# A transformer block on one core: products of probabilities and values in pairs, full-width transposes of the maxima, and a new order of stages

## The reference

```
x = x + 0.5 * ffn(layernorm(x))
x = x + attn(layernorm(x))
x = x + 0.5 * ffn(layernorm(x))

attn: q = rope(x @ Wq + bq); k = rope(x @ Wk + bk); v = x @ Wv + bv
      out = softmax(q k^T / 4) v per head; out @ W0 + b0
ffn:  base = x @ W_base + b_base
      h_n = relu(x @ W_enc[n] + b_enc[n]); recon_n = h_n @ W_dec[n] + b_dec[n]
      n* = argmin over n of mean((recon_n - x)^2)
      mid = relu(x @ W_down[n*] + b_down[n*]); out = base + mid @ W_up[n*] + b_up[n*]
```

## Time and profile before

| | |
|---|---|
| median of 3 runs | 1844.04 us (1842.85 to 1847.05) |
| the profiled execution | 1842.72 us |
| its span on the core | 1840.9 us |
| mean granted TensorE clock | 0.976 |
| PE busy | 1739.8 us |
| DVE busy | 1286.3 us |
| ACT busy | 978.3 us |
| POOL busy | 497.6 us |

### The profile page before, as it was taken

How to read it: one execution, slowest core, us unless ns; L and a number is a source line. 1 busy time by engine, 2 the same in 40 slices (tenths; PEclk the granted TensorE clock), 3 DMA queues, 4 the chain that set the end, 5 groups by cost and what they waited for, 6 DMA issues and landing times.

```text
span 1840.9 us, 26466 instructions
## 1 busy us (share of the span) xinstructions
PE 1739.8 (95%) x9128; PEld 987.3 (54%) x9128; DVE 1286.3 (70%) x2795; ACT 978.3 (53%) x1954; POOL 497.6 (27%) x665
## 2 busy tenths in 40 slices
PE   6478999999999999999999999999999999999976
PEld 4343555555555555555556555555556555554434
DVE  5459686867768676776868677686867768686521
ACT  1126465655646565564646556474655637465531
POOL 2415041231414123141413214050322405032101
PEclk9689999999999999999999999999999999999996
DMA  4334231233333123333322333332233333214000
GB/s 117 58 59 79 43 52 37 45 69 58 70 58 53 38 41 67 58 70 58 58 36 51 54 59 69 58 61 39 52 46 58 70 58 61 46 41 69 18 12 12
DMA packets 96715, 99.38 MB, mean 54 GB/s; under 512 B 19972, under 2 KB 88261, under 8 KB 96453
## 3 DMA queue, kind: packets, MB, share of 16 engines
q1 hardware_dynamic: 93830, 97.16, 29.9%
q10 hardware_dynamic: 2752, 0.54, 0.2%
HBM read 63.54 MB, written 33.55 MB: 53 GB/s over the span
## 4 chain that ended last, share of the span: by engine, by line
PE 81%; DVE 11%; issue 2%; ACT 2%; DMA 2%; POOL 1%; SPq 0%; POOLq 0%; ACTq 0%; DVEq 0%
PE ps L725 11%; PE ps L784 10%; PE ps L737 10%; PE ps L713 10%; PE ps L800 10%; PE ps L802 6%; PE ps L842 5%; PE ps L858 4%; DVE mx L1088 4%; PE ps L843 3%; PE ps L824 3%; PE ps L868 2%; PE ps L769 2%; DVE xn L1119 2%; PE ps L889 1%
## 5 line engine op out<-in xcount | busy, mean ns | idle before, releaser
L1088 DVE TENSOR_REDUCE mx<-ps 128x1 f32<-128x512 f32 x1024 | 656.8, 683 | 287.2 <-PE ps L713 284.9
L940 ACT ACTIVATE pr<-ps 128x512 f32<-128x512 f32 x1024 | 556.2, 597 | 543.0 <-PE ps L725 541.9
L725 PE MATMUL ps<-stack 98*128 98x512 bf16 x1024 | 312.5, 384 | 7.9 <-ACT pr L940 2.4
L713 PE MATMUL ps<-stack 96*128 96x512 bf16 x1024 | 310.9, 381 | 4.7 <-DVE mx L1088 4.1
L737 PE MATMUL ps<-pr,va 128*32 128x512 f32 x2048 | 273.3, 604 | 1.2 <-ACT pr L940 1.1
L725 PEld LDWEIGHTS ps<-stack 98*128 98x128 bf16 x1024 | 73.9, 98 | 234.8 <-issue 158.1
L713 PEld LDWEIGHTS ps<-stack 96*128 96x128 bf16 x1024 | 99.0, 98 | 136.1 <-DVE mx L1088 30.6
L1315 POOL CAST wdh<-wd_all 128x128 fp32r x32 | 9.5, 296 | 555.9 <-DVE adapter L1169 499.9
L1141 DVE SCALAR_TENSOR_TENSOR ps<-ps,wb,h 128x512 f32<-128x512 f32 x128 | 96.8, 756 | 77.0 <-PE ps L802 76.9
L1250 POOL TENSOR_SCALAR rs<-mv 128x4 f32<-128x4 f32 x48 | 11.5, 239 | 471.6 <-DVE mv L1108 467.7
L1279 POOL TENSOR_TENSOR qb<-qb,cst 128x512 f32<-128x512 f32 x64 | 98.6, 1541 | 136.9 <-DVE qs L1195 136.9
(11 more groups left out here) (151 smaller groups left out, 2991.9 us busy)
## 6 DMA issues: line engine op xcount, KB each, us to landing
stack<-scratch SPq DMA_DIRECT2D x384, 128.0 KB, 6.1
scratch<-parts SPq DMA_DIRECT2D x64, 384.0 KB, 2.6
xin<-in_L_attn_x_dram SPq DMA_DIRECT2D x16, 512.0 KB, 4.4
out_dram<-x SPq DMA_DIRECT2D x16, 512.0 KB, 5.2
stack<-wu_mT SPq DMA_DIRECT2D x128, 4.0 KB, 1.7
cst<-in_const_dram SPq DMA_DIRECT2D x1, 1024.0 KB
raw<-in_L_ffn_W_dec_dram ACTq DMA_DIRECT2D x1, 512.0 KB, 5.6
pr<-in_L_ffn_W_enc_dram SPq DMA_DIRECT2D x2, 256.0 KB, 7.7
```

What stands on the lines that cost most here:

```text
L713: pe.matmul(bank1[:, t % 2, :], stack[0][0:KB, hd, 128 * t:128 * t + 128], stack[1][0:KB, hd, :], start=True, stop=True).then_inc(s1_full. ...
L725: pe.matmul(bank2[:, a % 2, :], stack[1][:, 4 * g + a, 128 * t:128 * t + 128], stack[0][:, 4 * g + a, :], start=True, stop=True).then_inc( ...
L940: act.activation(pr[:, n % 2, a, :], bank2[:, a % 2, :], ACT.Exp, scale=SCALE).then_inc(ex_done.sem, 1)
L1088: dve.tensor_reduce(mx[:, hd // 4 % 2, e:e + 1], bank1[:, t % 2, :], AX.X, ALU.max).then_inc(mx_done.sem, 1)
```

## The change

- `pv` m does tiles 2m and 2m+1 in one visit, 16 records, and signals once. `pr` holds three tiles, by a running number modulo 3.
- `mt` transposes 128 columns: the 32 columns of maxima lie beside the bf16 identity in one tile `mx_id`, at one end or the other, and ACT reads 32 partitions of the result.
- `cost` has one matmul in place of two; DVE adds `zt` to `z` behind the last `gr`.
- The squares go into `xl`, which is written with its own values later, and `xl` waits for `xT_done` (the squares) in place of `xh_done`. The normalised x of the attention part, `xn[2]`, is `xn[0]`.
- All five lists are in a new order: there are eight `pv` per batch, at other places; `en` +1,0,1 moves to the end of the round before; `gr`, `mt`, `tr`, `va`, `qk` shift by a place or two; on DVE one half of a normalisation goes ahead of output projection 0, and both halves of `lx` +2,0 ahead of head 13's second half.

```diff
     stage("up", +1, 0, 1)
+    stage("s1", 0, 7, 0)
     stage("st", +1, 2, 0)
     stage("st", +1, 2, 1)
-    stage("s1", 0, 7, 0)
     stage("s1", 0, 7, 1)
     stage("ms", 0, 1)
+    stage("lx", +1, 2, 0)
     stage("op", -1, 0)
-    stage("lx", +1, 2, 0)
+    stage("s1", 0, 8, 0)
     stage("lx", +1, 2, 1)
-    stage("s1", 0, 8, 0)
     stage("op", -1, 1)
...
+    stage("ro1", +1, 3)
     stage("s1", 0, 13, 0)
-    stage("ro1", +1, 3)
     stage("lx", +2, 0, 0)
+    stage("lx", +2, 0, 1)
     stage("s1", 0, 13, 1)
     stage("gr", -1, 1, 0)
-    stage("lx", +2, 0, 1)
...
-        xn = [sb(f"xn{s}", [128, T, D]) for s in range(3)]
+        xn = [sb(f"xn{s}", [128, T, D]) for s in range(2)]
+        xn.append(xn[0])
...
-        mx2 = sb("mx2", [128, 2, 2, 4 * T], BF16)
-        pr = sb("pr", [128, 2, 4, S])
+        mx_id = sb("mx_id", [128, 128 + 64], BF16)
+        ident_b = mx_id[:, 32:160]
+        mx2 = [mx_id[:, 160 * o:160 * o + 32].rearrange("p (a b) -> p a b", a=2) for o in range(2)]
+        pr = sb("pr", [128, 3, 4, S])
...
+        def held(b, n):
+
+            return pr[:, (b.number * G * T + n) % 3]
...
-                pe.wait_ge(*ex_done.at(b, 4 * n + 3))
-                for a in range(4):
-                    last = pe.matmul(bank_o[32 * a:32 * a + 32, :], va[b.odd][:, t, 4 * g + a, :], pr[:, n % 2, a, :],
-                                     start=(t == 0), stop=(t == T - 1))
+                pe.wait_ge(*ex_done.at(b, 8 * m + 7))
+                for n in (2 * m, 2 * m + 1):
+                    t = n % T
+                    for a in range(4):
+                        last = pe.matmul(bank_o[32 * a:32 * a + 32, :], va[b.odd][:, t, 4 * g + a, :], held(b, n)[:, a, :],
+                                         start=(t == 0), stop=(t == T - 1))
                 last.then_inc(pv_done.sem, 1)
...
-                pe.transpose(bank[0:32, 0:64].bitcast(BF16), mx2[:, g % 2, :, :].rearrange("p a b -> p (a b)"),
-                             ident_b[:]).then_inc(mt_full.sem, 1)
+                pe.transpose(bank[:, 0:64].bitcast(BF16), mx_id[:, 64 * (g % 2):64 * (g % 2) + 128], ident_b).then_inc(mt_full.sem, 1)
...
-                pe.wait_ge(*z_step[f].at(b, 4))
                 pe.wait_ge(*zm_done[f].at(b, 0))
-                pe.matmul(bank[0:32, 0:N], ones, zt[f][:, 0, :], start=True, stop=False)
-                pe.matmul(bank[0:32, 0:N], ones, z[f][:], start=False, stop=True).then_inc(cost_full[f].sem, 1)
+                pe.matmul(bank[0:32, 0:N], ones, z[f][:], start=True, stop=True).then_inc(cost_full[f].sem, 1)
...
-                    act.wait_ge(*pv_done.at(b, n - 2))
+                    act.wait_ge(*pv_done.at(b, (n - 3) // 2))
...
-                    act.copy(xh[s][:, c, :], bank).then_inc(xh_done[s].sem, 1)
-                    act.activation(squares[:, s, c, :], bank, ACT.Square, accum_out=sxx[s][:, c:c + 1]).then_inc(xT_done[s].sem, 1)
+                    act.copy(xh[s][:, c, :], bank)
+                    act.activation(xl[s][:, c, :], bank, ACT.Square, accum_out=sxx[s][:, c:c + 1]).then_inc(xT_done[s].sem, 1)
...
+                    dve.wait_ge(*z_step[f].at(b, 4))
+                    dve.sem_inc(passed, 1)
+                    dve.wait_ge(*zr_done[f].at(b, 0))
+                    dve.tensor_tensor(z[f][:], z[f][:], zt[f][:, 0, :], ALU.add).then_inc(zm_done[f].sem, 1)
...
-                    pool.wait_ge(*xh_done[1].at(b, c))
+                    pool.wait_ge(*xT_done[1].at(b, c))
```

More of the change, by code:

```diff
@@ L116, in tensor_order @@
     stage("s1", 0, 1, 0)
-    stage("pv", -1, 11)
+    stage("pv", -1, 5)
     stage("s2", -1, 12, 1)
@@ L126, in tensor_order @@
     stage("gr", +1, 0, 2)
-    stage("pv", -1, 12)
     stage("s2", -1, 14, 0)
     stage("s1", 0, 3, 0)
+    stage("gr", +1, 0, 3)
     stage("dn", -2, 1)
@@ L163, in tensor_order @@
     stage("ot", -1)
-    stage("pv", 0, 1)
     stage("s2", 0, 2, 1)
     stage("s1", 0, 7, 1)
+    stage("pv", 0, 0)
     stage("op", -1, 0)
@@ L202, in tensor_order @@
     stage("mt", 0, 2)
-    stage("pv", 0, 6)
+    stage("qk", +1, 2)
     stage("en", -1, 1, 1)
@@ L208, in tensor_order @@
     stage("en", -1, 1, 2)
+    stage("pv", 0, 3)
     stage("s2", 0, 8, 0)
@@ L262, in scalar_order @@
     stage("s2", 0, 2, 1)
+    stage("s2", 0, 3, 0)
     stage("mt", 0, 1)
-    stage("s2", 0, 3, 0)
     stage("s2", 0, 3, 1)
@@ L313, in vector_order @@
     stage("s1", 0, 0, 1)
+    stage("s1", 0, 1, 0)
     stage("pick", -2, 1)
-    stage("s1", 0, 1, 0)
     stage("s1", 0, 1, 1)
@@ L358, in vector_order @@
     stage("s1", 0, 9, 1)
+    stage("s1", 0, 10, 0)
     stage("ro1", +1, 0)
-    stage("s1", 0, 10, 0)
     stage("s1", 0, 10, 1)
@@ L366, in vector_order @@
     stage("va", +1, 1)
-    stage("ro3", +1, 0)
     stage("ms", 0, 2)
     stage("s1", 0, 12, 0)
+    stage("ro3", +1, 0)
     stage("st", +2, 0, 0)
@@ L412, in gpsimd_order @@
     stage("ro2", +1, 3)
+    stage("pick", -1, 1)
     stage("b0", +1)
-    stage("pick", -1, 1)
     stage("zs", +2, 0)
+    stage("pick", +2, 0)
+    stage("rs", +2, 2)
+    stage("rs", 0, 1)
 def sync_order(stage):
@@ L447, in walk @@
 def walk(order, do):
-    for number in range(-2, B + 2):
+    for number in range(-3, B + 2):
         def stage(name, ahead, *args):
@@ L578, in macaron @@
         xn_done = [sig(f"xn_done{s}", T) for s in range(3)]
-        xh_done = [sig(f"xh_done{s}", C) for s in range(2)]
         xl_done = [sig(f"xl_done{s}", C) for s in range(3)]
@@ L584, in macaron @@
         z_step = [sig(f"z_step{f}", 5) for f in range(2)]
+        zr_done = [sig(f"zr_done{f}", 1) for f in range(2)]
         zm_done = [sig(f"zm_done{f}", 1) for f in range(2)]
@@ L1116, in normalise @@
                         dve.wait_ge(*ot_full.at(b - 2, C - 1))
+                    else:
+                        dve.wait_ge(*tr_full[2].at(b - 1, C - 1))
                     dve.wait_ge(*rs_done[s].at(b, 0))
```

147 lines of the change are left out of this document (65 added, 82 removed).

## The result

The changed kernel takes 1822.63 us (median of 4 runs, 1820.51 to 1825.84) against 1844.44 us for the kernel before (4 runs, 1842.85 to 1847.05), a ratio of 0.9882 with a 95% interval of 0.9862 to 0.9902. The forecast was 1822 us. The sum was right; two of its parts were not, and they cancelled.

A forecast was written before the change was run, and what follows sets the result against it. PE's stream was taken to bound the rounds. 1.70 + 0.10 - 0.05 - 0.25 = 1.50 us, 14 rounds: 21; +1.7 and -1.3 make -21.4 on 1842.72: 1821.3; median 1.3 higher: 1822 us, range 1806 to 1836.

The forecast's parts named there:

- What bounds the kernel: Whole kernel: in the rounds only a shorter PE stream pays; in the last 136 us the last batch's chain sets the end.
- Pairs, 1.70: Products of probabilities and values, two per visit to the 32-column strips: saves 1.70 us a round.
- the term of the visits, 1.47: Eight of sixteen strip visits a round vanish, each saving 0.09 entry and 0.093 way back: 1.47 us.
- the other 0.23: Slower steps of matmuls that follow a product: 0.48 us a round before, some 0.25 after.
- rival 2: Inside each pair the second product waits for its weight loads, 0.16 us per pair, 20.5 us: 1842; chance 0.06.
- The full-width mt, +0.10: Maxima transpose over 128 columns needs no strips: gains 0.1 us a round, bounds -0.1 and +0.4.
- Cost, -0.05: Cost stage: one matmul less saves 0.06 twice, but one cost makes its own strip visit; net loss 0.05 us a round.
- The order, -0.25: New stage order: PE's waits grow 0.2 us a round to 1.6, plus 0.05 for DVE at head 13.
- Rival 1: DVE takes the gain back: waits grow by 0.8 to 1.5 us a round, 1828 to 1840; chance 0.15.
- rival 3: Slower: DVE's slowed normalisation halves hold head 13's maxima and PE over 1.7 us a round; 1856 at 2.5; chance 0.07.
- The last two stretches, -1.7: Stretches of 89 and 77 us after the full rounds: products there save 1.7 us, though part is bound by chains.
- Start and tail, +1.3: Chains at start and end: later xl behind the squares, 0.6 twice, and DVE's added step make the kernel 1.3 us longer.

The follow-up runs named there:

- e6: The kernel before with only the full-width transpose of the maxima added; 1848.62 us, ratio 1.0022 to the kernel before.
- e3: The changed kernel with the maxima transposed in a 32-column strip again, as before the change; 1831.87 us, ratio 0.9923 to the kernel before.
- e5: The changed kernel with two matmuls in the cost stage again and no addition on DVE; 1828.6 us, ratio 0.9907 to the kernel before.
- e11: The changed kernel with 17 extra matmuls that nothing reads, in TensorE's gaps in the last two batches; 1818.08 us, ratio 0.9853 to the kernel before.
- e4: The changed kernel with squares written back into their PSUM bank and xl waiting for xh alone; 1824.24 us, ratio 0.9891 to the kernel before.
- e13: e11 with five more extra matmuls and both halves of batch 14's second-layer transposes earlier on ScalarE; 1821.46 us, ratio 0.9885 to the kernel before.
- e8: The changed kernel with product pair 5 ahead of the scores of tile 12 in the last two batches only; 1819.53 us, ratio 0.9869.
- e1: The changed kernel with product pair 5 ahead of the scores of tile 12 in every batch; 1831.11 us, ratio 0.9923 to the kernel before.

## Why the prediction was right, and where two of its steps failed

- *What bounds the kernel*: right. Rounds follow the length of PE's stream (104.19 of 104.30 us busy), and going by starts was what made the small terms visible.
- *Pairs, 1.70*: measured 1.8 net (2.0 by starts, of which 0.25 turn into a wait for xl). The entry was right (0.10); the saving inside a pair was taken as the way back alone, 0.093, and is 0.14, since the third and fourth pass also come 0.43 after the one ahead in place of 0.45. So the term of the visits, 1.47, was too small by 0.5; the other 0.23 of the 1.70, for what follows a product, depends on the order, and no run shows it by itself.
- *Loads bare inside a pair (rival 2)*: refuted. The Trainium skill's page "TensorE: Matmul & The Clock Gate" (Part 3, The mechanism) lets loads overlap only where the row group differs, in its list of what overlaps; the sentence above its figure also allows it for loads into the background weight buffer. Here the loads of a pass that shares all rows with the one streaming take 0.13 us for four, beside it, and the step to the next product is 0.43. The trace does not agree with the list; with the sentence it can be reconciled, though no row here shows which buffer a load goes to.
- *The full-width mt, +0.10*: the step was priced as if its surroundings stayed. Alone in the old order it is -0.17 (e6), in the new order +0.58 (e3). That two of the four ride with a product was seen, and charged with a load of 0.05; what they pay in the old order is a step of their own, 0.14 and 0.23 with the broken visit. The bounds, -0.1 and +0.4, missed on both sides.
- *Cost, -0.05*: about right. The one matmul less is worth 0.06 twice, as forecast, and 0.15 a round in all (e5). In the new order the stage costs 0.16 by itself, twice, where it cost 0.22 by itself and 0.12 in company before.
- *The order, -0.25*: by steps, PE's waits came to 1.3 us a round instead of 1.6 (0.30 at a gram, 0.25 at the scores behind the first query projection, 0.24 at that projection, 0.18 and 0.14 at mt 1 and mt 2, some 0.17 at the transposes). The largest part was to be the query projection, 0.9 us, measured 0.24. The count named the half of a normalisation that moves ahead of the stretch, 0.85 us, and then left DVE at 8.7, its length before, instead of taking it off. The row at 1069.23 is that half, done before DVE's addition for output projection 0 at 1070.15; DVE's chain is 8.1 and PE's own work 7.9, and 9.1 - 0.85 = 8.25 would have said so. The wait in the kernel before was misread as well: the step of 0.97 was set against 0.44, which is usual ahead of scores, but ahead of a projection 0.26 is, so that 0.71 was waited in place of 0.53. Rival 1 and rival 3, which rested on the same counts, did not come: there is no wait at head 13. What the forecast did not count in the order are the new wait at the scores, 0.25, and the two pieces of `va`, 0.17; the lost company it had put into the mt and cost terms.
- *The last two stretches, -1.7*: this step failed by 9.6 us. The forecast wrote that part of them is bound by chains and then carried the saving of the rounds into them. In them no work of a next batch fills the gaps, so the places of the stages count more than their sum. 3.6 us come from the clock (shown by e11); the other 4.3 stay with the order by exclusion (e4 puts 0.2 of the last stretch on xl), and the encoder's late start is their visible part. Which move of the order it is stays open.
- *Start and tail, +1.3*: the tail grew by 0.8, of which 0.3 is xl behind the squares (e4); the start by 1.3, within what it varies from trace to trace. The tail varies too: e6, with the old order, has 56.4 where the kernel before has 58.6, and e13 has 56.8 where the changed kernel has 59.4. In both, the granted clock is 0.90 or more in the window from 48 to 54 us into the tail, where all the others have 0.50. So 0.8 from two single traces is weak evidence.

That the time came out at 1822 is luck in part: 10 us too little in the rounds against 10 us too much in the drain. The forecast's own terms, 1821.3 and 1.3, add up to 1822.6 and not 1822, which changes nothing.

## What to carry to other kernels

Price a small operation by the visit it makes, with the neighbours that it has in the new order: the same form of a transpose was worth 0.58 us a round in one order and cost 0.17 in the other. In a software pipeline, forecast the last rounds from their own timeline, since what fills a gap in a full round is missing there. Where an engine must wait for a DMA in the drain, look at the clock behind the wait: matmuls without a reader can be cheaper than the idle time.

## What the runs showed of the hardware that was not expected

- Four column strips that share all 128 rows go from pass to pass in 0.43 us with new weights in each, 0.45 from the first to the second.
- A wait of TensorE of 1.0 to 2.2 us in a sparse stretch was followed by three windows of 6 us at a mean clock between the levels 1.2 and 2.4 GHz (0.64, 0.78, 0.73), and where it falls differs between kernels whose stages there are alike: 84.8 us (e8) against 81.2 (e1) for one stretch. In e3 and e5 the clock falls in the stretch before the last too (0.57 and 0.59), and that stretch is 2.8 and 3.8 us longer than in the changed kernel. That is about as much as the smaller edits are worth.
- A wait alone does not say whether the clock falls: in the last stretch of the kernel before, PE waited 1.10 us for the same DMA and the clock's mean over the stretch stayed 1.00.
